# One Strassen level for the relation and gate-x products of a graph network, weights split block by block

## The reference, cut to what matters

```python
u = x @ root + bias
for r in range(8):
    sums = segment_sum(x[src] * mask_r, dst)
    u = u + (sums / max(count_r, 1)) @ weight[r]
z = concatenate([u, x]) @ w_gate + b_gate
h = tanh(u) * z + x * (1 - z)
x = layernorm(x + h)
```

## Time and profile before

| | |
|---|---|
| median of 3 runs | 1009.89 us (1009.81 to 1010.46) |
| profiled execution, first to last instruction | 1008.0 us |
| TensorE matmuls busy | 925.5 us (92%) |
| VectorE, ScalarE, POOL busy | 478.0, 336.0, 17.9 us |
| mean granted TensorE clock | 0.972 |
| chain that ended last | 84% TensorE, 7% VectorE, 3% DMA |

### The profile page before, as it was taken

How to read it: one execution, slowest core, us unless ns; L and a number is a source line. 1 busy time by engine, 2 the same in 40 slices (tenths; PEclk the granted TensorE clock), 3 DMA queues, 4 the chain that set the end, 5 groups by cost and what they waited for, 6 DMA issues and landing times.

```text
span 1008.0 us, 14165 instructions
## 1 busy us (share of the span) xinstructions
PE 925.5 (92%) x5387; PEld 478.4 (47%) x5388; DVE 478.0 (47%) x880; ACT 336.0 (33%) x456; POOL 17.9 (2%) x46
## 2 busy tenths in 40 slices
PE   0569999899999999999999999999999999999990
PEld 0556777645444444444444444444444444444440
DVE  3589998595533333243243243233333323344881
ACT  0693445455234232132222323213223213128100
POOL 1000001000000000000000000000000000000000
PEclk9788999899999999999999999999999999999995
DMA  4401000230302220220121022022022022010010
GB/s 154 129 3 48 1 0 1 89 141 25 139 28 84 84 84 1 84 84 14 70 83 48 35 83 81 2 83 83 0 104 83 0 83 84 17 67 1 21 43 39
DMA packets 28895, 58.06 MB, mean 58 GB/s; under 512 B 1322, under 2 KB 4530, under 8 KB 28850
## 3 DMA queue, kind: packets, MB, share of 16 engines
q1 hardware_dynamic: 28849, 57.46, 16.3%
HBM read 54.90 MB, written 2.56 MB: 57 GB/s over the span
## 4 chain that ended last, share of the span: by engine, by line
PE 84%; DVE 7%; DMA 3%; issue 2%; ACT 1%; DVEq 0%; SPq 0%; POOL 0%; ACTq 0%; POOLq 0%
PE psP L712 55%; PE psA L870 17%; PE psP L674 6%; PE psA L712 4%; DMA x<-in_x 3%; PE psP L788 1%; PE psA L663 1%; DVE stats L1186 1%; DVE wsplit L1013 1%; DVE p_mem L1035 1%; DVE wsplit L1106 1%; ACT wsplit L402 0%; DVE p_mem L1337 0%; DVE x L1208 0%; DVE p_mem L1339 0%
## 5 line engine op out<-in xcount | busy, mean ns | idle before, releaser
L712 PE MATMUL psP<-wsplit,xT 128*128 128x512 f16 x2400 | 521.6, 379 | 0.8 <-DVE u_mem L1251 0.8
L712 PEld LDWEIGHTS psP<-wsplit,xT 128*128 128x128 f16 x2400 | 234.8, 98 | 282.9 <-DVE u_mem L1251 1.3
L1233 DVE SCALAR_TENSOR_TENSOR p_mem<-psP,p_mem 128x512 f16<-128x512 f32 x80 | 55.3, 691 | 283.9 <-ACT p_mem L598 282.4
L598 ACT ACTIVATE p_mem<-psP 128x512 f16<-128x512 f32 x80 | 47.8, 597 | 403.1 <-PE psP L712 403.1
L870 PE MATMUL psA<-p_mem,c_mem 128*128 128x512 f16 x800 | 175.4, 379 | 1.4 <-DVE u_mem L1251 1.4
L870 PEld LDWEIGHTS psA<-p_mem,c_mem 128*128 (+1 forms) x800 | 78.2, 98 | 96.0 <-DVE u_mem L1251 1.9
L1251 DVE SCALAR_TENSOR_TENSOR u_mem<-psA,coef,u_mem 128x512 f32<-128x512 f32 x80 | 60.0, 751 | 101.6 <-PE psA L870 101.6
L1013 DVE SCALAR_TENSOR_TENSOR wsplit<-stage,sc,wsplit 128x4096 f16<-128x4096 f32 (+1 forms) x22 | 97.4, 4429 | 9.3 <-ACT wsplit L444 9.3
L674 PE MATMUL psP<-p_mem 125*128 125x140 f16 x1125 | 78.9, 233 | 24.0 <-DVE p_mem L1035 15.9
L674 PEld LDWEIGHTS psP<-p_mem 125*128 125x128 f16 x1125 | 76.0, 102 | 28.5 <-issue 15.6
L444 ACT ACTIVATE wsplit<-stage,sc 128x4096 f16<-128x4096 f32 (+1 forms) x22 | 80.6, 3663 | 23.2 <-DVE sc L936 18.6
(11 more groups left out here) (151 smaller groups left out, 364.5 us busy)
## 6 DMA issues: line engine op xcount, KB each, us to landing
stage<-in_L_gnn_weight SPq DMA_DIRECT2D x16, 2048.0 KB, 7.8
stage<-in_L_gnn_w_gate SPq DMA_DIRECT2D x4, 2048.0 KB, 7.7
stage<-in_L_gnn_W_rel SPq DMA_DIRECT2D x4, 572.0 KB, 11.7
x<-in_x SPq DMA_DIRECT2D x1, 2048.0 KB
xT<-in_L_gnn_root SPq DMA_DIRECT2D x1, 2048.0 KB, 7.9
stage<-in_L_gnn_root SPq DMA_DIRECT2D x1, 2048.0 KB, 8.0
out<-x SPq DMA_DIRECT2D x4, 512.0 KB
stage<-in_L_gnn_W_root SPq DMA_DIRECT2D x2, 572.0 KB, 13.3
```

The costliest lines, as they stand in the source:

```text
L598: nc.scalar.activation(p_part[slot][0][:, t, :], psP[:, t, :], ACT.Copy, scale=PROD_GAIN).then_inc(p_hi, 1)
L712: last = nc.tensor.matmul(out, lhs[:, a, c, bass.ts(t, P)], w[:, c, cols], start=first, stop=(c == chunks - 1 and a == 1))
L1233: ins = stt(p_part[slot][1][:, t, :], src, PROD_GAIN, p_part[slot][0][:, t, :], ALU.mult, ALU.subtract)
```

## The change

For the 16 relation units and the 2 gate-x units, the four full tiles are taken as 2 x 2 blocks A (256 nodes by 512 features) and the unit as 2 x 2 blocks B (512 by 256). Seven block products in Winograd's form take the place of eight; the fifth tile is multiplied as before, with the raw blocks. The sums of x (S1 to S4) are made once, during the root products: three lie where x was, which is kept in DRAM meanwhile (`x1_home`), one takes the place of a block of `xT`. The sums of the weights (T1 to T4, `first_diffs`, `third_diff`, `fourth_diff`) are made per unit on VectorE in fp32 and then split.

The weights are split in 1,024-element blocks into a ring of 8, in the order B11, T2, B21, T1, T3, T4, B12, B22; unit j + 1's block n is written after unit j's product n (`prod`). The absolute sum has four pieces, which POOL reduces together and VectorE adds up. The products gather in five banks; VectorE and ScalarE combine them through `p1_tmp`, `p16_tmp` and `c22`, while TensorE adds further products into the same banks (`p1_ready`, `p16_ready`, `c22_ready`). Root and gate-u units are split into the same ring without sums (`raw_high`, `raw_low`, `raw_product`: 512 columns from two blocks). The gate-x units run like the relations, with `gate_first`, `gate_16`, `gate_11`, `gate_22`, `gate_21`, `gate_12` (one to three 512-element passes each) for the combinations, and no rests; in the last of them, two transpositions of u stand before the last block's products (`first_turns`), and ScalarE's first emptying of them behind the splits and sums of gate-u.

```diff
+FB = HALF // 2
+KB = DC // 2
+RING_W = 8
+STEPS = 8
+B11, T2, B21, T1, T3, T4, B12, B22 = range(STEPS)
+SEVEN = U_GU - U_REL
...
+def weight_blocks(i):
+    if isinstance(i, int) and i < U_REL:
+        return 4 * (i - U_ROOT)
+    if isinstance(i, int) and i >= U_GU:
+        return 8 + STEPS * SEVEN + 4 * (i - U_GU)
+    return 8 + STEPS * (i - U_REL)
...
-        wsplit = sb("wsplit", [P, 2, 2, DC * HALF], F16)
+        wsplit = sb("wsplit", [P, RING_W, 2, KB * FB], F16)
...
+        TDIFF = {T1: 1, T2: 2, T4: 3, T3: 4}
...
+            sp.wait_ge(wsum_ready, 5)
+            load(U_REL, 0, w1_v[:, 0:DC, 0:HALF])
+            for t in range(NT):
+                sp.wait_ge(x1_ready, t + 1)
+                sp.dma_start(x1_home[:, t, :], x[:, t, :]).then_inc(x1_kept, 16)
+            sp.wait_ge(wlo_ready, weight_blocks(U_REL))
+            load(U_REL + 1, 1, w1_v[:, 0:DC, HALF:D])
+            with sp.Fori(1, R1) as r:
...
+            sp.wait_ge(p_lo, 5 * 2 * R1)
             sp.dma_start(vec[:, :], bg_d.partition_broadcast(P)).then_inc(gate_bias_loaded, 16)
-            for k, top in ((U_GX, D), (U_GU, 0)):
-                for h in range(2):
-                    load(k + h, h, by_chunk(wg_d[top:top + D, h * HALF:(h + 1) * HALF]))
+            load(U_GU, 0, by_chunk(wg_d[0:D, 0:HALF]))
+            load(U_GU + 1, 1, by_chunk(wg_d[0:D, HALF:D]))
+            sp.wait_ge(prod, STEPS * SEVEN)
+            sp.wait_ge(wlo_ready, weight_blocks(U_GU))
+            for t in range(NT):
+                sp.dma_start(x[:, t, :], x1_home[:, t, :]).then_inc(x1_back, 16)
...
+            def weight_sum(i, slot, loads):
+                act.wait_ge(stage_full[slot], loads)
+                st = stage_of(i, slot)
+                for n in range(4):
+                    part = slice(n * KB * FB, (n + 1) * KB * FB)
+                    if isinstance(i, int) and i < U_REL:
+                        act.wait_ge(w_used, 1 + slot)
+                        land = sp_mem[:, (8 * slot + n) * KB * FB:(8 * slot + n + 1) * KB * FB]
+                    else:
+                        act.wait_ge(wsum_ready, 4 * (i - U_ROOT) + n + 1)
+                        land = p_land
+                        if not (isinstance(i, int) and i < U_REL + 2):
+                            act.wait_ge(p_lo, 5 * (2 * R1 - 1) + 2 if isinstance(i, int) and i >= U_GU - 1 else 5 * (i - U_REL - 2) + 2)
+                            land = key_mem[:, :].bitcast(F16)
+                    nc.scalar.activation(land, st[:, part], ACT.Abs,
+                                         accum_out=am[:, slot, n:n + 1]).then_inc(wsum_ready, 1)
...
+            def raw_high(i, slot):
+                act.wait_ge(scale_step, 4 * i + 4)
+                for n, (k, f) in enumerate(RAW):
+                    b = weight_blocks(i) + n
+                    if i >= U_GU:
+                        act.wait_ge(prod, STEPS * (SEVEN - 1) + b % RING_W + 1)
+                    nc.scalar.activation(split_block(b % RING_W, 0), raw_block(i, slot, k, f), ACT.Copy,
+                                         scale=sc_f[:, scale_col(i, slot), 2:3]).then_inc(whi_ready, 1)
...
+            def step_high(j, slot, n, first=False):
+                if first:
+                    act.wait_ge(root_full, NT if n < 4 else 2 * NT)
...
+                    act.wait_ge(prod, STEPS * (j - 1) + n + 1)
+                if n in TDIFF:
+                    act.wait_ge(tdiff_ready, 4 * j + TDIFF[n])
+                nc.scalar.activation(split_block(n, 0), step_block(REL, slot, n), ACT.Copy,
+                                     scale=sc_f[:, scale_col(REL, slot), 2:3]).then_inc(whi_ready, 1)
...
+            weight_sum(U_REL, 0, slot_load(U_REL))
+            act.wait_ge(x1_kept, 16 * NT)
+            for n, ready in ((0, 1), (1, 3), (2, 4)):
+                act.wait_ge(stot_ready, ready)
+                nc.scalar.activation(s_mem[:, n, 0, :, :], s_tot[n], ACT.Copy).then_inc(s_hi, 1)
+            act.wait_ge(scale_step, 4 * U_REL + 4)
+            for n in range(4):
+                step_high(0, 0, n, first=True)
+            weight_sum(U_REL + 1, 1, slot_load(U_REL + 1))
+            act.wait_ge(stot_ready, 4)
+            act.wait_ge(root_full, 2 * NT)
+            nc.scalar.activation(xT[:, 0, 0:KB, 2 * P:4 * P], s_tot[3], ACT.Copy).then_inc(s_hi, 1)
+            for n in range(4, STEPS):
+                step_high(0, 0, n, first=True)
+            act.wait_ge(rcnt_ready, 1)
+            def bank(n):
+                return psP[:, n, :].rearrange("p (t f) -> p t f", t=2)
+            def rel_step(j, slot, loads, settled=True, ahead=True):
+                hi = p_part[slot][0]
+                def high(dst, src, gain=1.0):
+                    nc.scalar.activation(dst, src, ACT.Copy, scale=gain).then_inc(p_hi, 1)
+                act.wait_ge(prod, STEPS * j + 1)
+                nc.scalar.activation(p1_tmp, bank(0), ACT.Copy, scale=PROD1_GAIN).then_inc(p1_ready, 1)
+                act.wait_ge(scale_step, 4 * (j + U_REL + 1) + 4)
+                step_high(j + 1, 1 - slot, 0)
+                step_high(j + 1, 1 - slot, 1)
+                act.wait_ge(prod, STEPS * j + 3)
+                if settled:
+                    act.wait_ge(agg_full, NT * (j - 1))
+                high(hi[:, 0:2, 0:FB], bank(0), PROD1_GAIN)
+                step_high(j + 1, 1 - slot, 2)
+                step_high(j + 1, 1 - slot, 3)
+                act.wait_ge(c22_ready, j + 1)
+                high(hi[:, 2:4, FB:HALF], c22[:, :, :])
+                step_high(j + 1, 1 - slot, 4)
+                act.wait_ge(c21_ready, j + 1)
+                high(hi[:, 2:4, 0:FB], p1_tmp)
+                step_high(j + 1, 1 - slot, 5)
+                step_high(j + 1, 1 - slot, 6)
+                act.wait_ge(prod, STEPS * (j + 1))
+                high(hi[:, 4, :], psP[:, 4, :], PROD1_GAIN)
+                act.wait_ge(c12_ready, j + 1)
+                high(hi[:, 0:2, FB:HALF], p16_tmp)
+                step_high(j + 1, 1 - slot, 7)
+                weight_sum(j + (U_REL + 2), slot, loads)
...
+            gate_first(0)
+            act.wait_ge(scale_step, 4 * (U_GX + 1) + 4)
+            for n in range(STEPS):
+                step_high(2 * R1 + 1, 1, n)
             weight_sum(U_GU, 0, slot_load(U_GU))
+            gate_first(1)
             act.wait_ge(row_scaled, 1)
             for t in range(NT):
                 nc.scalar.activation(us[:, t, :], u[:, t, :], ACT.Copy, scale=rows_f[:, 1, 2, t:t + 1]).then_inc(us_ready, 1)
+            raw_high(U_GU, 0)
+            weight_sum(U_GU + 1, 1, slot_load(U_GU + 1))
             split_hi(2, 0, uT, 1.0)
-            weight_hi(U_GU, 0)
-            weight_sum(U_GU + 1, 1, slot_load(U_GU + 1))
             split_hi(2, 1, uT, 1.0)
...
+            def seven(j, settled, late=None):
+                def part(n, bank, col, lhs, first, done=False):
+                    for tt in range(len(lhs)):
+                        for c in range(KB):
+                            for a, b in ((0, 0), (0, 1), (1, 0)):
+                                last = nc.tensor.matmul(psP[:, bank, (col + tt) * FB:(col + tt + 1) * FB], lhs[tt](a, c),
+                                                        split_block(n, b)[:, c, :],
+                                                        start=(first and tt == 0 and c == 0 and a == 0 and b == 0),
+                                                        stop=False, skip_group_check=True)
+                    return last
...
+                S3, S2, S4 = range(3)
+                Z, X, Y, W, V = range(NT)
+                b0 = weight_blocks(U_REL + j)
+                settled()
+                blocks_ready(b0 + 1)
+                part(B11, Z, 0, x_tiles(0, 0, 1), True)
+                if isinstance(j, int) and j == 0:
+                    pe.wait_ge(root_done, 2 * NT)
+                part(B11, V, 0, x_tiles(0, 4), True).then_inc(prod, 1)
+                if isinstance(j, int) and j == 0:
+                    pe.wait_ge(s_lo, 3)
+                blocks_ready(b0 + 2)
+                part(T2, X, 0, s_tiles(S2), True).then_inc(prod, 1)
+                blocks_ready(b0 + 3)
+                pe.wait_ge(p1_ready, j + 1)
+                part(B21, Z, 0, x_tiles(1, 0, 1), False)
+                part(B21, V, 0, x_tiles(1, 4), False).then_inc(prod, 1)
+                if isinstance(j, int) and j == 0:
+                    pe.wait_ge(s_lo, 4)
+                blocks_ready(b0 + 4)
+                part(T1, Y, 0, x_tiles(0, 2, 3), True).then_inc(prod, 1)
+                blocks_ready(b0 + 5)
+                pe.wait_ge(p16_ready, j + 1)
+                part(T3, X, 0, s_tiles(S3), False).then_inc(prod, 1)
+                blocks_ready(b0 + 6)
+                part(T4, W, 0, x_tiles(1, 2, 3), True).then_inc(prod, 1)
+                blocks_ready(b0 + 7)
+                part(B12, V, 1, x_tiles(0, 4), False).then_inc(prod, 1)
+                if late:
+                    late()
```

(142 more changed lines are left out.)

413 lines of the change are left out of this document (256 added, 157 removed).

## The result

The changed kernel takes **1049.28 us** (median of 4, 1047.41 to 1049.61) against 1010.17 (4 runs, 1009.81 to 1010.81): ratio **1.038** [1.037, 1.040], slower, as forecast; the forecast of 1057 was 8 us too high. The profiled execution is the shortest of the four; its span of 1045.5 us is 37.5 above the 1008.0 before.

The account below looks back on a forecast made before the run. TensorE was taken to bound the kernel. Stages 6.6 + 7.3 + 2.8 - 0.7 + 14.6 = 30.6 on a 1008.0 span, plus 1.9 around it, gave 1040.5; clock falls added 17: 1057 us, range 1022 to 1084.

Parts of the forecast that it names:

- The mechanism and the stages: VectorE's accumulations come late, TensorE stands 2.8 us per aggregation; start +6.6, periods +7.3, last stall +2.8, unit 16 -0.7, gate +14.6.
- hidden after all: Rival: loop chain from product 3 takes 18.0 us or less, so no stall; 998, or 983 with gate harmless; chance 0.13.
- the matmuls bind: Rival: products of 256 columns take 120 ns, saving nothing; period 38.2, 1055 us with the clock held; chance 0.04.
- the signs it named: Aggregation gap 2.8 from VectorE's accumulation, period 37 to 39, products 109 ns, gate-x gap 12 to 14, clock under 1.0 often.
- the clock: TensorE's granted clock falls to half after stops; 10 falls at 1.7 us each add 17 us.
- 15 stalls of 2.8 us: TensorE's waits in the aggregations; half of them were taken to lose the clock, at 1.7 us each.
- the two long ones: Stops of 5.8 us before unit 1 and 4.0 us in unit 16, both taken to lose the clock.
- Late, but the clock holds: Rival: TensorE stalls in the loop but keeps full clock; 1040 us (1030 to 1046), chance 0.25.
- the case with falls: Likeliest case: TensorE stalls and the clock falls at some stops; 1057 us (1046 to 1075), chance 0.43.
- dearer: Rival: over 30 VectorE waits per unit cost 0.05 each, 1.5 us per period; 1061, or 1078 with clock; chance 0.12.
- the start: Up to the first aggregation: slower weight sums and a wait before unit 1, +6.6 us.
- The gate: Unit 17 to gate-u: late row maxima and ScalarE's queue put gate-u at P + 43.3 against 28.7 before, +14.6 us.

Follow-up runs that it names:

- run 1: Changed kernel with VectorE's first accumulation moved ahead of the combination of product 8 and the second ahead of low 7: 1003.27 us.
- run 5: Changed kernel with row maxima and scales ahead of unit 17's first two evacuations, and ScalarE's second gate-u weight sums behind the turned tiles' splits: 1041.44 us.
- run 6: Changed kernel with only the row maxima and scales moved ahead of unit 17's first two evacuations: 1042.41 us.
- run 7: Changed kernel with all of run 5, and VectorE's low parts of the first two turned tiles ahead of its raw lows: 1037.66 us.
- run 3: Changed kernel with two unused VectorE maxima passes ahead of the first accumulation of each of 15 aggregations: 1112.83 us.
- run 4: Changed kernel with one unused VectorE maxima pass ahead of the first accumulation of each of 15 aggregations: 1101.63 us.

## Why the prediction was right, and where it was off

**The mechanism and the stages** were right, and run 1 shows the main one: the 2.3 us that seven products save per unit (216 x 109.2 ns; the weight loads stay hidden) were more than eaten by a stop of 2.9 us, because VectorE kept the accumulations behind a chain through three engines. With the order changed and the same work, the saving appears at 34.4 us per period. The rival "hidden after all" was refuted at S = 2.9, "the matmuls bind" by 109.2 ns. Of the signs it named all came but one: the gap of 2.9 us put down to VectorE's accumulation, the period of 37.55, products 109 ns apart and a TensorE gap of 13.1 us before the last gate-x block, but not a granted clock under 1.0 in many periods.

**The step that failed is the clock**: "15 stalls of 2.8 us lie among the stops that lost it. I take half of the 15, and the two long ones [...]: 10 x 1.7 = 17." None of the 15 fell in the profiled execution, nor did the one in unit 16 (it did in the profiles of five runs); of those counted in the 17 only the 5.65 us stop ahead of unit 1 did, 2.3 us. The same 15 stops kept the clock in the profiles of runs 5, 6 and 7 too. "Late, but the clock holds", at 0.25, was what happened in the loop. That 1049 still lies inside the 1046 to 1075 given for the case with falls is luck: that case did not occur, and the one fall at the start, the periods below and the 1.9 us of the median above the profiled execution carried the time there. The evidence came from the counting stage, with other matmuls ahead of the stop; runs 3 and 4 show the price real at 4.1 us and more, where it was 1.9 and 2.2 us on average. The Trainium skill (TensorE: Matmul & The Clock Gate, Why this matters for your kernels) warns that a gap between bursts of matmuls that is long enough takes TensorE back to half clock. The runs agree for the 30 stops of 4.1 us and more; the 15 of 2.9 to 3.1 did not do it here.

**The smaller errors.** A period is 37.55, not 37.2: 0.14 in the chain up to TensorE's restart, 0.15 because the 30 matmuls behind the stop took 6.65 us for 6.5, and six of the 15 stops, every second one inside the loop, are 3.11 instead of 2.93. Over 14 periods that is 4.7 us, a quarter of what the "dearer" rival asked for (1.5 each). And the start cost 8.3, not 6.6: 2.3 is the clock, counted there in the 17; without it the walk was 0.6 too high. So 1057.5 (1040.5 + 17) - 14.7 (clock) + 4.7 (periods) - 0.6 (start) + 0.5 (behind gate-u's start) = 1047.4, the profiled execution's time. The median is 1.9 above that. The likeliest reason is unit 16's stop, whose fall costs 1.7 in four of the five profiles that show one: the other three executions have a mean granted clock of 0.962 or 0.963 against 0.965. They have no trace, so this is argued and not shown.

**The gate** was right to 0.1 us, but run 5 shows how little a right sum says of what a repair will bring: once the first queue is out of the way, the next one (VectorE's raw lows) holds the same step.
